# Selective scan of a four-layer network: in chunks 5 to 10 TensorE multiplies dt*u by B for 8 of 32 states

## What is computed

```python
dt = softplus(einsum(dt_r, dt_proj_w) + dt_proj_b)     # (b, s, 512)
A = -exp(A_log)                                        # (512, 16)
def step(h, inp):                                      # for each token t
    dt_t, B_t, C_t, u_t = inp
    h = h * exp(dt_t[:, :, None] * A) + (dt_t * u_t)[:, :, None] * B_t[:, None, :]
    y = einsum('bdn,bn->bd', h, C_t)
    return h, y
```

## Time and profile before

| | us |
|---|---|
| median of 3 runs (2170.87 to 2171.65) | 2170.93 |
| the profiled execution: its own time | 2168.83 |
| its span, first to last instruction | 2166.9 |
| VectorE busy, whole span | 1857.6 (86%) |
| TensorE busy | 1744.4 (81%) |
| POOL busy | 1150.6 (53%) |
| ScalarE busy | 1197.1 (55%) |

### The profile page before, as it was taken

How to read it: one execution, slowest core, us unless ns; L and a number is a source line. 1 busy time by engine, 2 the same in 40 slices (tenths; PEclk the granted TensorE clock), 3 DMA queues, 4 the chain that set the end, 5 groups by cost and what they waited for, 6 DMA issues and landing times.

```text
span 2166.9 us, 22530 instructions
## 1 busy us (share of the span) xinstructions
PE 1744.4 (81%) x7648; PEld 588.7 (27%) x7648; DVE 1857.6 (86%) x2189; ACT 1197.1 (55%) x2143; POOL 1150.6 (53%) x584
## 2 busy tenths in 40 slices
PE   6586988769798777878687878786897799999986
PEld 2121322223132111222221112232662333333323
DVE  2688999899999999999999999999548588888813
ACT  2646565554656556555565656553450366666672
POOL 2467878777889877878888786864000000000000
PEclk9798998968788788878778778797995799999998
DMA  5142222222222222222222222331060162220001
GB/s 194 38 145 65 75 75 73 63 70 69 74 69 82 76 78 75 80 65 77 65 78 79 75 82 75 103 91 46 1 119 0 59 90 33 31 31 2 2 2 39
DMA packets 80727, 143.41 MB, mean 66 GB/s; under 512 B 14587, under 2 KB 19643, under 8 KB 80076
## 3 DMA queue, kind: packets, MB, share of 16 engines
q1 hardware_dynamic: 80612, 141.98, 23.7%
HBM read 132.34 MB, written 9.01 MB: 65 GB/s over the span
## 4 chain that ended last, share of the span: by engine, by line
DVE 46%; PE 34%; issue 10%; ACT 5%; POOL 3%; DMA 1%; SPq 1%; DVEq 0%; ACTq 0%; POOLq 0%
DVE hbuf L2139 26%; DVE hbuf L2124 11%; PE psum L682 6%; PE psum L1579 4%; PE psum L668 4%; DVE gain L958 4%; PE psum L648 4%; PE psum L563 3%; PE psum L1413 3%; POOL hbuf L1326 2%; PE psum L552 2%; PE psum L1389 1%; PE psum L1558 1%; PE psum L1440 1%; PE psum L1535 1%
## 5 line engine op out<-in xcount | busy, mean ns | idle before, releaser
L1326 POOL TENSOR_TENSOR hbuf<-hbuf,cbuf 128x1024 f32<-128x1024 f32 x384 | 902.6, 2358 | 292.8 <-DVE hbuf L2139 146.4
L1931 ACT ACTIVATE psum<-slots,cols 128x512 f32<-128x512 f32 x768 | 525.3, 687 | 459.3 <-DVE hbuf L2139 456.6
L1579 PE MATMUL psum<-hbuf,ident 64*64 64x512 f32 x3072 | 524.4, 760 | 212.9 <-POOL hbuf L1326 212.6
L2124 DVE TENSOR_TENSOR hbuf<-slots,psum 128x1024 f32<-128x1024 f32 x384 | 458.7, 1195 | 21.9 <-PE psum L1558 21.8
L2139 DVE TENSOR_TENSOR_SCAN hbuf<-psum,hlast,hbuf 128x512 f32<-128x512 f32 x384 | 470.2, 1265 | 3.1 <-ACT psum L1931 3.0
L2139 DVE TENSOR_TENSOR_SCAN hbuf<-psum,hbuf 128x512 f32<-128x512 f32 x384 | 446.9, 1203 | 3.2 <-ACT psum L1931 3.1
L958 DVE TENSOR_REDUCE gain<-psum 128x1 f32<-128x512 f32 x512 | 314.6, 682 | 74.3 <-PE psum L648 74.0
L513 POOL COPY wl<-hbuf 128x512 f32<-128x512 f32 x8 | 4.9, 616 | 443.1 <-PE psum L682 414.5
L648 PE MATMUL psum<-slots 99*128 99x512 bf16 x512 | 212.5, 419 | 25.3 <-DVE gain L970 13.1
L1558 PE MATMUL psum<-bcs,pick 48*128 48x512 bf16 x384 | 170.1, 443 | 52.9 <-DVE hbuf L2124 50.8
L668 PE MATMUL psum<-slots 102*128 102x512 bf16 x512 | 194.8, 388 | 6.4 <-ACT xn_flat L839 1.7
(11 more groups left out here) (261 smaller groups left out, 1954.4 us busy)
## 6 DMA issues: line engine op xcount, KB each, us to landing
cbuf<-scr_c SPq DMA_DIRECT2D x384, 256.0 KB, 3.1
slots<-scr_qk SPq DMA_DIRECT2D x96, 128.0 KB
scr_qk<-slots SPq DMA_DIRECT2D x10, 512.0 KB, 2.8
wl<-in_w SPq DMA_DIRECT2D x1, 3968.0 KB, 12.6
wl<-in_ada_w SPq DMA_DIRECT2D x1, 3584.0 KB
xt<-in_x SPq DMA_DIRECT2D x2, 1024.0 KB, 12.1
wl<-in_w SPq DMA_DIRECT2D x2, 1024.0 KB, 6.5
out<-xt SPq DMA_DIRECT2D x2, 1024.0 KB, 4.6
```

Of the source, the lines that this page charges most:

```text
L1326: pool.tensor_tensor(hs, hs, cbuf[:, at % CRING:at % CRING + 1, :].to_broadcast([P, 2, TC]), ALU.mult).then_inc(weighed, 1)
L1579: last = pe.matmul(psum[side, bank, :], ident[rows_of, rows_of], hbuf[rows_of, at % RING, q, :], start=False, stop=n == NS - 1, skip_group ...
L1931: act.activation(decay_bank(at, q), dts[k % 2][:, e, :], ACT.Exp, scale=coefficient(WORK[k], e, n)).then_inc(decay, 1)
L2124: dve.tensor_tensor(hbuf[:, at % RING, :, :], ws[k % 2][:, 2 * p:2 * p + 2, :], psum[:, 2 + at % 2:3 + at % 2, :].to_broadcast([P, 2, TC]) ...
```

## The change

In chunks 5 to 10 the states 6, 8, 10 and 12 of both tile pairs, 8 of 32 slots, have no `spread` and no `load`. Instead

- dt*u is turned to time-major once per chunk: `turn_w` (TensorE, four transposes per channel tile, slots 2, 3 and 14 to 16) and `turned_w` (ScalarE copies to `wT`, slots 4, 5 and 15 to 17);
- `store_diagonals` (SP, slot 26 of the chunk before, behind the three DMAs of B) writes the four rows of B into `scr_diag` in HBM, each value at its own place on the diagonals of 128 x 128 blocks; `load_diagonals` (slot 0) reads the blocks into `diag_b`. A DMA in chunk 1 clears `scr_diag`;
- `product(at, q)` makes (dt*u)*B as four f32 matmuls of 128 x 128 x 128 in a PSUM bank: tile 0 in bank 2 or 3, tile 1 in bank 7, after the scan before it has read that bank;
- the decays of these slots go to the ring `hbuf` and the scan takes its inputs from PSUM.

`b_left` and `in_two` move a remainder to another buffer, with as many elements as before.

```diff
+PE_CHUNKS = range(5, NK - 1)
+PE_STATES = (6, 8, 10, 12)
...
+            def store_diagonals(k):
+                for i, n in enumerate(PE_STATES):
+                    on_diagonal = scr_diag[k % 2, i:i + 1, :].rearrange("a (t x) -> a t x", x=TC + 1)[:, :, 0:TC]
+                    on_diagonal = on_diagonal.rearrange("a t (j p) -> a j t p", p=P)[:, :, :, 0:1]
+                    values = xp_out[RANK + n:RANK + n + 1, :].rearrange("a (j t o) -> a j t o", t=P, o=1)
+                    sp.dma_start(on_diagonal, values, allow_slow_non_contiguous=True).then_inc(diag_stored, 16)
+
+            def load_diagonals(k):
...
+                for i in range(len(PE_STATES)):
+                    src = scr_diag[k % 2, i, 0:P * TC].rearrange("(t m) -> t m", m=TC)
+                    sp.dma_start(diag_b[i], src).then_inc(ld_diag[i], 16)
...
                 if j + 1 < NK:
                     yield 26
                     spread_inputs(j + 1)
+                if j + 1 in PE_CHUNKS:
+                    sp.wait_ge(diag_cleared, 16)
+                    store_diagonals(j + 1)
...
+            def turn_w(k, e):
+
+                pe.wait_ge(w_ready, k * KE + e + 1)
+                ps = begin("wT", k, e)
+                for i in range(TB):
+                    last = pe.transpose(ps[:, i * P:(i + 1) * P], ws[k % 2][:, e, i * P:(i + 1) * P], ident[:, :])
+                last.then_inc(grouped, 1)
+
+            def product(at, q):
...
+                pe.wait_ge(taken_act, taken(G["wT", k, 2 * p + q]))
+                pe.wait_ge(ld_diag[i], 16 * (k - PE_CHUNKS[0] + 1))
+                if q:
+                    pe.wait_ge(scanned, 2 * (at - 1) + 2)
+                else:
...
+                    pe.wait_ge(dbu, loaded(before))
+                    if by_matmul(at - 2):
+                        pe.wait_ge(scanned, 2 * (at - 2) + 1)
+                for j in range(TB):
+                    last = pe.matmul(product_bank(at, q)[:, j * P:(j + 1) * P], wT[:, j, q * P:(q + 1) * P], diag_b[i][:, j * P:(j + 1) * P],
+                                     start=True, stop=True)
+                last.then_inc(dbu_matmul, 1)
...
-                    if at + 2 < TOTAL:
+                    if by_matmul(at - 1) and not by_matmul(at + 1):
+                        spread(at + 1)
+                    if by_matmul(at):
+                        product(at, 1)
+                    elif at + 2 < TOTAL and not by_matmul(at + 2):
                         spread(at + 2)
                     if at >= 2:
                         add_state(at - 2)
+                    if by_matmul(at + 1):
+                        product(at + 1, 0)
...
+                elif by_matmul(at):
+                    act.wait_ge(summed, at - RING + 1)
...
-                    if at + 1 < TOTAL:
+                    if at + 1 < TOTAL and not by_matmul(at + 1):
                         load(at + 1)
```

More of the change, by code:

```diff
@@ L96, with by_matmul, loaded, multiplied @@
 N_LAST = sum(len(n) for n in NORM.values())
+PE_CHUNKS = range(5, NK - 1)
+PE_STATES = (6, 8, 10, 12)
+def by_matmul(at):
+    k, h = divmod(at, HALVES)
+    return k in PE_CHUNKS and h % NS in PE_STATES
+def loaded(at):
+    return sum(not by_matmul(n) for n in range(at + 1))
+def multiplied(at):
+    return sum(by_matmul(n) for n in range(at + 1))
 def head_groups(k):
@@ L103, in head_groups @@
     elif c.backward:
-        names = [("z", KE), ("ahead", 2), ("u", KE)]
+        names = [("z", KE), ("ahead", 2), ("wT", KE), ("u", KE)]
     else:
         names = [("u", KE)]
-    return [(name, k, i) for name, count in names + [("xp", 1), ("dt", 2)] for i in range(count)
-            if k or name != "ahead"]
+    groups = [(name, k, i) for name, count in names + [("xp", 1), ("dt", 2)] for i in range(count)
+              if k or name != "ahead"]
+    return [("wT", k - 1, i) if name == "wT" else (name, k, i) for name, k, i in groups
+            if name != "wT" or (k - 1 in PE_CHUNKS and i >= 2)]
 def turn_groups(k):
@@ L121 @@
         GROUPS += [("dt", _j, e) for e in (2, 3)]
+    if _j in PE_CHUNKS:
+        GROUPS += [("wT", _j, e) for e in (0, 1)]
     if _first:
@@ L134 @@
     if _k in FRESH and not _first:
+        if _j in PE_CHUNKS:
+            GROUPS += [("wT", _j, e) for e in (2, 3)]
         GROUPS += turn_groups(_k)
@@ L312, in build, with in_two @@
         wf1 = wl1[:, W1_F:NW1].rearrange("p (k m) -> p k m", k=KE)
+        wT = wl1[:, W1_Z:W1_Z + TB * D].rearrange("p (j e) -> p j e", j=TB)
+        diag_b = [wl1[:, a:a + TC] for a in (W1_C + KD * DI, W1_C + KD * DI + TC, W1_C + 3 * KD * DI, W1_C + 3 * KD * DI + TC)]
+        no_b = wl23_flat[:, 3584:3584 + (TC + 1) // 3]
+        b_left = wdts[RANK:RANK + NS, 0:2, TC // 2:TC]
+        def in_two(rows):
+            return rows.rearrange("r (a t) -> r a t", a=2)
         def own_rows(k):
@@ L352, in build @@
         bcast, dbu, decay = sem("bcast"), sem("dbu"), sem("decay")
+        no_b_ready, diag_cleared, diag_stored = sem("no_b_ready"), sem("diag_cleared"), sem("diag_stored")
+        ld_diag, dbu_matmul = [sem(f"ld_diag{n}") for n in range(len(PE_STATES))], sem("dbu_matmul")
         scanned, weighed, summed = sem("scanned"), sem("weighed"), sem("summed")
@@ L1465, in head @@
                             from_x("z", k, e, wx1, e * P)
+                        if k - 1 in PE_CHUNKS:
+                            yield 16
+                            for e in (2, 3):
+                                turn_w(k - 1, e)
                     for e in range(KE):
@@ L1481, in beside @@
                         steps_of(j, e)
+                if j in PE_CHUNKS:
+                    for e in range(2):
+                        yield 2 + e
+                        turn_w(j, e)
                 if first:
@@ L1503, in beside @@
                 if k in FRESH and not first:
+                    if j in PE_CHUNKS:
+                        yield 14
+                        for e in (2, 3):
+                            turn_w(j, e)
                     yield 15
@@ L1553, in spread @@
                 n = h % NS
-                if at >= 2:
-                    pe.wait_ge(dbu, at - 1)
+                before = max((m for m in range(at % 2, at, 2) if not by_matmul(m)), default=None)
+                if by_matmul(at - 2):
+                    pe.wait_ge(scanned, 2 * (at - 2) + 1)
+                elif at >= 2:
+                    pe.wait_ge(dbu, loaded(before))
                 if h == 0:
@@ L1876, in beside @@
                     step_exp(j, 3)
+                    if j in PE_CHUNKS:
+                        turned_w(j, 0)
                     yield 5
+                    if j in PE_CHUNKS:
+                        turned_w(j, 1)
                     if first:
@@ L1903, in beside @@
                         folded_weights(d)
+                    if j in PE_CHUNKS:
+                        yield 15
+                        for e in (2, 3):
+                            turned_w(j, e)
                     yield 16
@@ L1910, in beside @@
                     silus(k)
+                    if j in PE_CHUNKS:
+                        yield 17
+                        for e in (2, 3):
+                            turned_w(j, e)
                 yield from head(k)
@@ L2120, in load @@
                     dve.wait_ge(w_ready, k * KE + 2 * p + 2)
-                dve.wait_ge(bcast, at + 1)
+                dve.wait_ge(bcast, loaded(at))
                 if at >= RING:
@@ L2133, in scan @@
                     dve.wait_ge(saved, (FIRSTS.index(k - 1) + 1) * HALVES)
-                dve.wait_ge(dbu, at + 1)
+                if not by_matmul(at):
+                    dve.wait_ge(dbu, loaded(at))
                 for q in range(2):
```

53 lines of the change are left out of this document (45 added, 8 removed).

## The result

| | before | after |
|---|---|---|
| median of the runs | 2170.9 us (2169.3 to 2171.7, 4 runs) | 2235.3 us (2231.5 to 2239.5, 4 runs) |
| span of the profiled execution | 2166.9 us | 2229.8 us |
| VectorE busy in the span | 86% | 81% |

The ratio is 1.0299 (95% interval 1.0287 to 1.0312), 64.4 us more. The forecast was 2193 (22 more). The sign was right; two thirds of the size are missing from its sum.

A forecast was written before the change was run, and what follows sets the result against it. VectorE was taken as the bound in chunks 5 to 10. Loads removed -53.8, TensorE and POOL +37, stores +39 gave +22: 2191 us profiled, 2193 median; eight in ten from 2145 to 2240.

The forecast's parts named there:

- loads and TensorE with POOL: Chunks 5 to 10: 48 loads removed from VectorE save 53.8 us; TensorE and POOL lateness gives back 37.
- stores of single values: Chunks 4 to 9: four stores ahead of slot 27's C delay it and VectorE's next first load, 39 us in sum.
- clearing and diagonal loads: Clearing scr_diag once is hidden, C being loaded three slots ahead; four loads behind slot 0 meet a late POOL: 0.
- The bound now: Chunks 5 to 10: VectorE is the bound without a gap, busy 675 of 676 us; TensorE and POOL have slack.
- POOL's 3.6 us per slot: Slots 4 to 7: POOL needs 3.6 us per slot against VectorE's 2.9, so is some 3 us late at slot 8.
- TensorE in its order: Slots 6 to 12: two slots want 6.2 us of TensorE against VectorE's 5.6 to 5.84, so TensorE becomes the bound there.
- Section one: Product slots 6 to 13: TensorE and POOL lateness costs 2 x 2.5 + 2 x 3 + 2 x 5 = 21 us.
- section two: Slots 21 to 29: the low-rank product between two products costs 2.2 us in four chunks, 3.5 in chunks 7 and 8: 16.
- Rival 4: Product slots: TensorE's clock stays at 0.9, costing 33 us in six chunks: 2226, or 2187 without the DMA term; chance 0.08.
- the rule for the number of engines: DMA stores: engines are the largest k up to 16 dividing both sides' slowest dimension: 4 here, 3 for `scr_ones`.
- the first sign that I named: Trace after: the last `scr_diag` store of a chunk lands after 10 to 12 us; under 4 under rival 1.
- Rival 3: Stores: single values cost 35 ns each, 88 us instead of 39, giving 2242 us; chance 0.15.

The follow-up runs named there:

- e2: The changed kernel without its DMA work (no clearing of scr_diag, stores, diagonal loads or waits for them), products multiplying whatever lies in the tiles: 2164.1 us.
- e1: The changed kernel with each store of 512 single values written as one plain row of 2 KB at the same place in the queue: 2181.4 us, ratio 1.0057.

## Why the prediction was right in sign and short in size

The measured pieces, each a run less the next, so that they must add up to the whole: loads gone with nothing in their place -21.5, products and transposes +15.0, clearing, plain rows and diagonal loads +17.3, single values instead of rows +54.0; sum +64.8. Against the forecast's terms:

| term | forecast | measured |
|---|---|---|
| loads and TensorE with POOL, -53.8 + 37 | -17 | -6.5 (e2) |
| stores of single values | +39 | +54.0 (after less e1) |
| clearing and diagonal loads | 0 | +17.3 (e1 less e2, with the plain rows) |

- **The bound now.** Right, and not enough. That VectorE is busy for 111.20 of 111.20 us says that it is the bound, not how far behind it the next one is. The prediction saw POOL's 3.6 us per slot and priced it as a part of the products' delay. This step failed. In fact it is a limit of its own: it takes away 18 us of the gain with no product there, and ScalarE some more.
- **TensorE in its order.** The arithmetic of 6.2 us for two slots held within 0.1: in chunks 5 and 6 product, spread, two `add_state` and a z projection follow each other every 6.25 us almost without a gap (in chunk 5 at 738.05, 744.30, 750.55 and, with one gap, 757.07). Section one was forecast at 21 and has 26.5 us of idle time in e2, section two at 16 and has 18.5. To both come 0.1 us for each of 47 stops, which no step of mine had. Chunk 9, at 6.0 instead of 3, and chunk 8, at 7.4 instead of 5, were underpriced most.
- **The clock in the product slots.** Rival 4 did not come: the rows below (slots 6 to 13 of chunk 5, 22 to 29 of chunk 6) have 0.96 and 1.00, above the 0.93 and 0.86 of the earlier trace rows. By the rule that the Trainium skill gives (TensorE: Matmul & The Clock Gate, "What's actually happening"), that activity releases the throttled default, the trace agrees. It agrees in the other direction too, which I did not use: behind the pauses of 4.5 to 10.3 us at the end of a chunk TensorE works at 0.50, in the kernel before as well.

```profile
734.50:760.50 26.00, 25.81 (x149) 11.97 (x147) 23.56 (x21) 14.08 (x22) 25.72 (x13) 0.96 0.25 79
906.00:931.00 25.00, 24.28 (x148) 11.50 (x146) 21.10 (x19) 17.38 (x34) 17.58 (x9) 1.00 0.18 48
```

- **The stores.** The chain was right in each link up to the first load: C of slot 27 late by 8.9 us in chunk 4 (6.61 of SP and 2.3 more to landing) against 9.7; POOL's wait 8.3 to 10.4 against about 8; the wait of the first load 40.0 us in six chunks against 39. The step that failed is the end of that list. The sum stopped at the first load, as if the stall were paid there, and the earlier trace rows, a stall inside a chunk, seemed to say so with its one row. Here four states stand behind the burst, and the waits for the spread and the decays bring 40 to 54. That the issues take 1.8 us was wrong too (6.61), but what SP waits the landing need not, and the sum of both is near. That it is near is partly luck. The 9.7 were four engines busy all the time at 19 ns a value, and the share of 0.08 to 0.14 shows only about two busy; no run shows the time of one value. My check of the rule for the number of engines was no better: a share of 0.08 is 1.3 engines, which fits three no more than four or sixteen. And the first sign that I named, the stores' time to landing, is not in the trace, which has none for them. Rival 3, values of 35 ns at 2242, came nearest in time, for a wrong reason.
- **The clearing.** "Hidden, as C is then loaded three slots ahead" was said without a sum. Three slots are 10 us; eight times the 256 KB of C, which land in 3.1 us, would have been 25, and it took 22.8. So this step, a term put at nothing without a sum, failed too. This was the easiest to avoid, and it cost some 10 us.
- **The diagonal loads** behind slot 0 were put at nothing; e1 and e2 leave them at most 4 us.

Of the 42 us that were missing, 15 are the second half of the stall, some 17 the clearing and the loads, and 10 the rest of POOL's and ScalarE's lateness.
